# Feed-forward stages of a macaron network: scaling by GpSimd, rounding constant by ScalarE, gate and up products released one by one

## What is computed

```python
def fp4_quant_dequant(x):                 # blocks of 16 along the last axis
    scale = max(max(abs(xb)) / 6.0, 1e-12)
    xn = xb / scale
    idx = searchsorted(_MID, abs(xn))     # nearest of 0, 0.5, 1, 1.5, 2, 3, 4, 6
    return _GRID[idx] * sign(xn) * scale

def fp4_linear(x, w):
    return einsum('bsk,nk->bsn', fp4_quant_dequant(x), fp4_quant_dequant(w))

def _L0_ffn_ref(x, w_gate, w_up, w_down):
    gate = fp4_linear(x, w_gate)          # 128 -> 352
    y = fp4_linear(x, w_up)
    h = silu(gate) * y
    return fp4_linear(h, w_down)          # 352 -> 128

x = x + 0.5 * _L0_ffn_ref(_layernorm(x), w_gate, w_up, w_down)
```

## Time and profile before

| | |
|---|---|
| median of three runs | 2275.11 us |
| the profiled execution's own time | 2278.47 us |
| its span, first to last instruction | 2276.7 us |
| mean granted clock of TensorE | 0.931 |
| TensorE busy | 1866.1 us (82%) |
| VectorE busy | 1669.5 us (73%) |
| ScalarE busy | 1066.1 us (47%) |
| GpSimd busy | 1080.2 us (47%) |
| the two feed-forward stages | 184.15 and 185.34 us |

### The profile page before, as it was taken

How to read it: one execution, slowest core, us unless ns; L and a number is a source line. 1 busy time by engine, 2 the same in 40 slices (tenths; PEclk the granted TensorE clock), 3 DMA queues, 4 the chain that set the end, 5 groups by cost and what they waited for, 6 DMA issues and landing times. The chain is left out here.

```text
span 2276.7 us, 36764 instructions
## 1 busy us (share of the span) xinstructions
PE 1866.1 (82%) x12205; PEld 1097.1 (48%) x12205; DVE 1669.5 (73%) x3322; ACT 1066.1 (47%) x2294; POOL 1080.2 (47%) x1304
## 2 busy tenths in 40 slices
PE   0555489999999999999935548999948888789999
PEld 0334234444444444444414435666637677656665
DVE  5887677888788877888778875666667777746665
ACT  0112255555555555555511135555537667445555
POOL 0111255555555555555611134555545556345555
PEclk9888599999999999999968977999979999879999
DMA  6000122222222222222100000000000000000000
GB/s 181 0 0 1 28 56 63 61 59 56 60 60 61 57 57 62 60 61 57 43 0 1 0 1 1 1 0 0 0 0 1 1 1 1 1 1 9 9 9 9
DMA packets 77058, 64.53 MB, mean 28 GB/s; under 512 B 12224, under 2 KB 75904, under 8 KB 76928
## 3 DMA queue, kind: packets, MB, share of 16 engines
q1 hardware_dynamic: 71392, 57.41, 9.9%
q10 hardware_dynamic: 5536, 5.52, 0.8%
HBM read 10.32 MB, written 2.10 MB: 5 GB/s over the span
## 5 line engine op out<-in xcount | busy, mean ns | idle before, releaser
L795 ACT ACTIVATE at_pT<-at_turned 128x512 f32<-128x512 f32 x512 | 305.6, 597 | 292.2 <-PE at_turned L862 273.3
L1022 POOL TENSOR_TENSOR m_g<-m_gT,m_g 128x512 f16<-128x512 f32 x260 | 301.4, 1159 | 232.1 <-ACT m_g L1005 232.1
L1036 PE MATMUL m_h<-m_xT,m_w 128*128 (+1 forms) x1572 | 386.8, 383 | 19.9 <-PEq L463 19.9
L694 DVE TENSOR_REDUCE at_nmax<-at_score 128x1 f32<-128x512 f32 x512 | 337.2, 680 | 71.8 <-PE at_score L839 68.7
L673 POOL TENSOR_TENSOR m_w_attn<-at_pT 128x512 f32<-128x512 f32 x128 | 162.4, 1269 | 377.1 <-ACT at_pT L795 377.1
L972 DVE TENSOR_TENSOR m_gT<-m_silu,m_h 128x512 f32<-128x512 f32 x262 | 180.3, 688 | 200.5 <-ACT m_silu L1001 200.4
L1001 ACT ACTIVATE m_silu<-m_h 128x512 f32<-128x512 f32 x262 | 156.6, 598 | 227.1 <-PE m_h L1036 227.1
L716 DVE RECIPROCAL m_w_attn<-m_w_attn 128x512 f32<-128x512 f32 x64 | 214.6, 3353 | 38.6 <-ACT m_w_attn L801 38.6
L900 PE MATMUL at_pv<-at_pT,at_v 128*64 128x512 f32 x1024 | 231.4, 594 | 0.0
L1055 PEld LDWEIGHTS m_y<-m_w,m_g 128*128 128x128 f16 x3072 | 192.9, 98 | 60.5
L1036 PEld LDWEIGHTS m_h<-m_xT,m_w 128*128 128x128 f16 x1572 | 144.3, 99 | 149.6 <-issue 28.3
(11 more groups left out here) (231 smaller groups left out, 3262.6 us busy)
## 6 DMA issues: line engine op xcount, KB each, us to landing
at_both<-at_part_q SPq DMA_DIRECT2D x128, 128.0 KB, 2.4
at_kh<-at_part_k SPq DMA_DIRECT2D x256, 64.0 KB, 2.0
at_both<-at_part_q SPq DMA_DIRECT2D x128, 64.0 KB, 2.0
at_kl<-at_part_k SPq DMA_DIRECT2D x128, 64.0 KB, 2.0
m_x<-in_x SPq DMA_DIRECT2D x8, 256.0 KB, 4.7
at_both<-at_mrow SPq DMA_DIRECT2D x128, 1.0 KB
out_x<-m_x SPq DMA_DIRECT2D x8, 256.0 KB, 2.3
m_wqkv<-in_w_qkv ACTq DMA_DIRECT2D x1, 1152.0 KB, 6.6
```

Source lines behind the costliest of these rows:

```text
L694: nc.vector.tensor_reduce(nmax[head][:, qt:qt + 1], score[use % 2][:], AX.X, ALU.max, negate=True)\
L795: nc.scalar.activation(pT[g % 2][:, head, kt, :], turned[i % 2][:], ACT.Exp).then_inc(exp_done, 1)
L1022: nc.gpsimd.tensor_tensor(g16[u % 4][:, 1, :], gT[u % 4][:], g16[u % 4][:, 0, :], ALU.subtract).then_inc(low_done, 1)
L1036: last = nc.tensor.matmul(bank[:], mem["w12_16"][:, w_part, e, first:first + P], mem["xT"][:, x_part, ds(b * SEQ, SEQ)], start=(i == 0), s ...
```

## The change

In both feed-forward stages:

- x is handled in ranges of two, two, and then seven times four tiles, with two or three buffers each, and no longer in groups of eight. All statistics of the layer norm come first.
- Normalising x, the product with the reciprocal of the scale and the product with the scale go to GpSimd (`normed`, `x_ratio`, `x_back`, `h_ratio`, `h_back`).
- VectorE keeps the largest value, the scale, its reciprocal and the exponent mask. ScalarE makes the constant's part above the floor, `relu(m * C - C)`, in place (`x_floor`, `h_floor`). VectorE then adds C + that part and removes it with two scalar_tensor_tensor steps (`x_round`, `h_round`).
- The gate product and the up product have a semaphore each; TensorE runs gates two units ahead, between the transposes of h and the way down, and ups behind the way down.
- The addition of unit n's result to x moves from one unit behind to three behind the current one.
- Semaphores of past stages are cleared on SyncE at the start of the feed-forward and norm stages.

```diff
 def ffn_stage(nc, mem, tag):
-    GT = UT * UPG
+    RANGES = [(0, 2), (2, 2)] + [(t, 4) for t in range(4, NT, 4)]
...
@@ vector queue @@
-                fp4_grid(nc, ch, h[:].rearrange("p t i -> p (t i)"), hg[i][:], hsc[i][:], w)
-                if v == 0 and g + 1 < GROUPS:
-                    x_part(g + 1, ch)
-                if n:
-                    add(n)
+                for n in range(UNITS + 1):
+                    if live(n):
+                        h_scales(n)
+                    if n:
+                        h_exponent(n - 1)
+                    if starts(n + 4):
+                        x_exponent(starts(n + 4))
+                    if live(n):
+                        h_inverse(n)
+                    if live(n + 1):
+                        gated(n + 1)
+                    if n:
+                        h_round(n - 1)
+                    if live(n - 3):
+                        add(n - 3)
+                    if starts(n + 4):
+                        x_round(starts(n + 4))
+                    if starts(n + 5):
+                        x_scales(starts(n + 5))
+                add(UNITS - 2)
+                add(UNITS - 1)
...
+                def h_round(n):
+                    i = n % 2
+                    dve.wait_ge(hr_done, n + 1)
+                    if n >= 2:
+                        dve.wait_ge(hq_done, n - 1)
+                    ch.link(nc.vector.scalar_tensor_tensor(out=hg[i][:], in0=hr[i][:], scalar=ROUND_TO_HALF, in1=hy[i][:],
+                                                           op0=ALU.add, op1=ALU.add))
+                    nc.vector.scalar_tensor_tensor(out=hg[i][:], in0=hg[i][:], scalar=ROUND_TO_HALF, in1=hr[i][:], op0=ALU.subtract,
+                                                   op1=ALU.subtract).then_inc(hg_done, 1)
...
@@ gpsimd queue @@
+                for n in range(UNITS):
+                    h_ratio(n)
+                    if starts(n + 3):
+                        x_back(starts(n + 3))
+                    if n:
+                        h_back(n - 1)
+                    if starts(n + 5):
+                        x_ratio(starts(n + 5))
+                        if starts(n + 5) + 1 < NR:
+                            normed(starts(n + 5) + 1)
...
@@ scalar queue @@
+                for n in range(UNITS + 1):
+                    if live(n + 2):
+                        silu_gate(n + 2)
+                    if live(n - 2):
+                        h_out(n - 2)
+                    if n:
+                        h_floor(n - 1)
+                    if starts(n + 4):
+                        x_floor(starts(n + 4))
+                    if starts(n + 3):
+                        x_out(starts(n + 3))
...
+                def h_floor(n):
+                    i = n % 2
+                    act.wait_ge(he_done, n + 1)
+                    nc.scalar.activation(hr[i][:], hr[i][:], ACT.Relu, bias=floor[:], scale=ROUND_TO_HALF).then_inc(hr_done, 1)
...
@@ tensor queue @@
-                    if n + 1 < UNITS:
-                        pe.wait_ge(h_done, n + 1)
-                        gate_up((v + 1) % UPG, (n + 1) // UPG % 2)
-                    if n:
-                        way_down(n - 1)
-                    if v == 1 and g + 1 < GROUPS:
-                        turn(g + 1)
+                    if live(n - 2):
+                        turn_back(n - 2)
+                    if live(n + 2):
+                        gates(n + 2)
+                    if live(n - 2):
+                        way_down(n - 2)
+                    if live(n + 2):
+                        ups(n + 2)
+                    if starts(n + 3):
+                        turn(starts(n + 3))
...
+                def way_down(n):
+                    i = n % 2
+                    pe.wait_ge(hqT_ready, n + 1)
+                    if n:
+                        pe.wait_ge(added, n)
...
@@ sync queue, in the feed-forward and norm stages @@
+            @block.sync
+            def _(sp):
+                for sem in mem["spent"]:
+                    sp.sem_clear(sem)
```

More of the change, by code:

```diff
@@ L283, in ffn_stage @@
         turn_x, down = s.bank("turn_x"), s.bank("down")
[L284 to L289, removed]
+        (chain, ln_ready, xn_done, xs_done, xy_done, xe_done, xr_done, xg_done, xq_done, x_turned, xqT_ready, gate_done,
@@ L290, in ffn_stage @@
+        blk = lambda a: a.rearrange("p (b k) -> p b k", k=BLK)
+        wide = lambda a: a.unsqueeze(2).to_broadcast([P, a.shape[1], BLK])
+        live = lambda n: 0 <= n < UNITS
+        NR = len(RANGES)
+        first_of = lambda r: RANGES[r][0]
+        x_wide = lambda r: RANGES[r][1] * P
+        x_blocks = lambda r: RANGES[r][1] * P // BLK
+        starts = lambda u: RANGE_OF[u] if live(u) and u >= 2 and u % 2 == 0 else None
         with nc.Block() as block:
+            @block.sync
+            def _(sp):
+                for sem in mem["spent"]:
+                    sp.sem_clear(sem)
@@ L292, in _ @@
             @block.vector
             def _(dve):
[L294 to L303, removed]
+                ch = Chain(dve, chain)
@@ L363, in h_out @@
                 def h_out(n):
                     act.wait_ge(h_turned, n + 1)
+                    if n >= 2:
+                        act.wait_ge(down_done, n - 1)
                     nc.scalar.copy(hqT[n % 2][:], turn_h[:, :, 0:INTER_PAD]).then_inc(hqT_ready, 1)
[L368 to L371, removed]
@@ L373, in _, with x_out @@
-                x_out(0, 0)
-                silu_gate(0)
-                for n in range(UNITS):
-                    if n + 1 < UNITS:
-                        act.wait_ge(h_done, n + 1)
-                        silu_gate(n + 1)
-                    if n:
[L380 to L383, removed]
+                def x_out(r):
+                    act.wait_ge(x_turned, r + 1)
+                    if r == 2:
+                        act.wait_ge(up_done, 1)
+                    elif r == 3:
+                        act.wait_ge(up_done, 2)
+                    elif r >= 4:
+                        act.wait_ge(up_done, 2 * (r - 2))
+                    nc.scalar.copy(xqT[r % 2][:, 0:x_wide(r)], turn_x[:, 0:x_wide(r)]).then_inc(xqT_ready, 1)
@@ L567, in _ @@
                         last.then_inc(l_done, 1)
+        mem["spent"] = s.sems
 def attn_stage(nc, mem, tag):
```

256 lines of the change are left out of this document (185 added, 71 removed).

## The result

The changed kernel takes 2334.16 us (median of four runs, 2333.01 to 2337.01) against 2274.52 for the kernel before beside it: ratio 1.0266, 95% interval 1.0248 to 1.0283. It is slower by 59.6 us. 2316 was forecast, 18 us too low, within the range of 2262 to 2342. The profiled execution took 2337.01 us with a span of 2335.2.

A forecast was written before the change was run, and what follows sets the result against it. The prediction took VectorE to bound the kernel before. A stage was 59 + 10 x 11.7 + 29 = 205 us against 184.15 and 185.34, together +40.6: 2316 us beside the median, range 2262 to 2342.

The forecast's parts named there:

- The ring: Circle of waits through TensorE, ScalarE and VectorE, from addition to addition: 9.66 us a unit, 11.7 with the clock lost.
- The clock: TensorE idles 4.7 us in each turn of the ring, losing its clock in most units: 2.0 us more a turn.
- signs: What would show the forecast: among others, gate and up matmuls spaced 1.2 us, granted clock near 0.7 or less.
- Start of a stage: From the stage's start to the end of the first addition: about 59 us, bounds 52 and 64.
- I take 0.3: Estimated price in us of a 128-wide tensor_scalar on GpSimd, normalising x, between rows of 0.198 and 1.27.
- End of a stage: After ten full rings, turns with fewer matmuls and the closing chain: together 29 us (26 to 31).
- closing chain: Last steps of a stage, taken over from the kernel before (213.36 to 220.61): 7.2 us.
- VectorE's need: VectorE's own work in the two feed-forward stages: 7.0 us a unit against 9.5, busy about 115 us a stage.
- the ring at 2.4 GHz: First rival: pauses do not lose TensorE's clock, a ring takes 9.66 us, 2271 us in all; chance 0.13.
- No ring: Rival: the order leaves slack, VectorE and GpSimd's shared pair binds at 7.9 to 9.1 us, 2238 to 2260; chance 0.08.
- The pair: Rival: a GpSimd product comes between VectorE's two rounding steps, a ring grows by 1.2 us, 2340 in all; chance 0.10.
- the fourth rival: TensorE's clock never comes back: 14.6 us a ring, 2374 us in all; chance 0.07.

The follow-up runs named there:

- e1: Changed kernel with VectorE's addition of unit n-3 placed before the rounding of unit n-1: 2257.87 us, 0.9928 of the kernel before.
- e4: Changed kernel with h's rounding constant back on VectorE instead of ScalarE, x's staying on ScalarE: 2256.99 us, 0.9919 of the kernel before.
- e9: Changed kernel with the floor of unit n-1 moved ahead of silu(n+2) and h_out(n-2) in ScalarE's queue: 2246.11 us, 0.9878 of the kernel before.
- e5: Changed kernel with x normalised by VectorE and not by GpSimd: 2326.06 us, 1.0200 of the kernel before.
- e2: Changed kernel with six more, unread up products per unit on TensorE between gates and the wait of the way down: 2288.22 us, 1.0057 of the kernel before.
- e6: Changed kernel with the edits of e1 and e4 together: 2254.15 us, 0.9880 of the kernel before.
- e8: Changed kernel with the edits of e1, e4 and e5 together: 2246.44 us, 0.9848 of the kernel before.
- e10: Changed kernel with the edits of e9, e1 and e5 together: 2228.05 us, 0.9799 of the kernel before.

## Why the prediction was right, and where it was off

- **The ring** was the right mechanism, and its mean length was right: forecast 11.7 us, measured 11.69 and 11.61 (single turns 10.55 to 12.82). e1, e4 and e9 each open it at another joint (the addition, the floor, the queue of ScalarE) and bring the spacing to 8.4 to 9.1. e5, which takes load off GpSimd and off no step of the ring, leaves it at 11.67.
- **The clock** was right: 2.1 us a turn (e2) against 2.0. The granted clock was 0.78 and 0.72 where I had said near 0.7 or less. As signs I had named gates and ups at half speed; it is the way down (2.90) and most of the ups (up to 2.55), and the gates of all ten turns take 1.35 to 1.45 us for four, at 2.4 GHz.
- **Start of a stage** was mis-sized: 59 forecast, 64.7 and 64.9 measured, above its upper bound of 64. The term that failed is GpSimd's normalising, "I take 0.3", which is 0.86. The bounds of 0.198 and 1.27 held it; I chose the end nearer to the 8-wide row since 128 columns of one input are a quarter of the other row's and half its reads. VectorE waits 8.0 us a stage for ten tiles normalised on GpSimd; ten times the 0.5 us between forecast and measured price, an estimate, is most of the 5.7 that were missing. e5 has 58.7 with the same work on VectorE.
- **End of a stage** was mis-sized: 29 forecast (26 to 31), 33.9 measured. The turns there hold fewer matmuls, and I let them run at 2.4 GHz for the most part. In the last 25 us no group of matmuls does (the granted clock is 0.57 from 225.34 to 250.34). The timeline of the changed kernel, and behind it the last two groups of the kernel before:

```profile
225.64 2.90 PE L612 MATMUL f_down<-m_wdT,f_hqT 128*128 128x128 f32 x12 [3.95 <-DVE m_x L389]
...
233.76 2.90 PE L612 MATMUL f_down<-m_wdT,f_hqT 128*128 128x128 f32 x12 [3.95 <-DVE m_x L389]
...
236.45 1.49 PE L600 MATMUL f_turn_h<-m_ident,f_hq 128*128 128x128 f32 x6
...
241.89 2.90 PE L612 MATMUL f_down<-m_wdT,f_hqT 128*128 128x128 f32 x12 [3.95 <-DVE m_x L389]
...
244.58 1.49 PE L600 MATMUL f_turn_h<-m_ident,f_hq 128*128 128x128 f32 x6
...
246.96 2.93 PE L612 MATMUL f_down<-m_wdT,f_hqT 128*128 128x128 f32 x12 [0.89 <-ACT f_hqT L526]
```

```profile
214.79 1.54 PE L414 MATMUL f_turn_h<-m_ident,f_hq 128*128 128x128 f32 x6 [3.12 <-POOL f_hq L349]
...
217.22 2.93 PE L422 MATMUL f_down<-m_wdT,f_hqT 128*128 128x128 f32 x12 [0.89 <-ACT f_hqT L366]
```

  Four times 1.32 us for the way down and three times 0.67 for the transposes are 7.3 us more than at 2.4 GHz. The closing chain of 7.2 us that I took over from the kernel before held 2.0 of it, since its last two groups already ran at 1.2 GHz. Set against the forecast, the first three turns took 9.03, 8.13 and 8.12 us where 8.5, 7 and 6.3 were forecast (3.5 more), and the closing chain 8.6 for 7.2 (1.4 more); together the 4.9 that were missing. In the closing chain it is the order on TensorE that costs: the last transposes stand behind the way down of the unit before and start at 244.58, 1.7 us after GpSimd's product has ended, where in the kernel before they waited for that product alone.
- **The sum**: 5.7 + 5.9 from the starts and 4.9 + 4.9 from the ends, less 1.0 for rings a little shorter than 11.7, make 20.4 us, and 20.3 were missing (60.9 measured, 40.6 forecast).
- **VectorE's need** was too low: 115 us a stage forecast, 126 measured. Its steps are stretched beside GpSimd (the 1.29 above), and GpSimd carries 5.6 us a unit and not 4.4. In its loop the changed kernel doesn't pay for that, as VectorE waits for 4.30 us in the turn shown. VectorE's busy time is what binds e6, e8 and e10.
- **The rivals**: the ring at 2.4 GHz is e2's loop, and it did not happen by itself. "No ring" fell for the changed kernel, but its price of 165 to 177 us a stage is near what e1, e4 and e9 then measured once they had opened it (169.1 to 178.2). The pair did not cut into the ring: L380 and L382 took 0.89 each in all ten full turns of the first stage. The clock came back in each turn of the loop, in time for the gates, so the fourth rival fell too, except in the last turns.
- The clears on SyncE were costed at nothing, and nothing shows of them: outside the two stages the span is 2.4 us shorter than before.

What stays open: how much of the 8.1 to 9.1 us at which the opened versions run is VectorE held off by GpSimd. A second bank for `down`, which would take the wait for the addition away by itself, was not tried; the stage has a use for each of the eight banks that it holds.

## What to carry to other kernels

When work moves off the busiest engine, write down for one period of the loop who waits for whom, across all queues, and look for a circle; where it is longer than what the busiest engine needs, its length is the new period, whatever the busy times say. A step that another engine waits for belongs at the place in its queue where its own input is ready, not behind steps of another unit: two lines moved up in ScalarE's queue were worth 88 us here. And a circle with a pause in it can cost twice, by its length and by TensorE's clock, which was worth 2.1 us of a turn of 11.7 here.

## What was not expected of the hardware

- On GpSimd a tensor_scalar with a mean and a factor per partition takes 0.78 us for 128 columns (3.12 for four, alone on the engine), more than a product of two inputs over 256 columns (0.62), and three quarters of one over 512 (1.06). VectorE needs 1.43 us for the same four.
- ScalarE's activation of 704 columns takes 0.89 us from SBUF to SBUF (the floor) and 0.76 from PSUM to SBUF (silu). Whether the function or the source makes the difference, no run here tells.
- VectorE and GpSimd hold each other off in both directions. In e1's timeline the 704-wide product waits for x's first rounding step, and the second step, 0.69 us by itself, then waits for the product:

```profile
126.02 0.69 DVE L342 SCALAR_TENSOR_TENSOR f_xg<-f_xr,f_xy 128x512 f32<-128x512 f32 x1
126.18 1.77 POOL L471 TENSOR_TENSOR f_hq<-f_hg,f_hsc 128x704 f32<-128x704 f32 x1 [1.75 <-DVE f_hg L382]
126.74 1.75 DVE L343 SCALAR_TENSOR_TENSOR f_xg<-f_xg,f_xr 128x512 f32<-128x512 f32 x1
```

  The product spans 1.77 us where 1.39 is its own time. The Trainium skill (SBUF — State Buffer, "SBUF: two separate sides") calls it an exclusive lock, held for a whole instruction; the trace agrees: 126.74 + 1.75 is 0.54 behind the product's end at 127.95, most of a step of 0.69.
